# Graph attention and gated expert FFN on one core: how the attention stage broadcasts its scores and sums its rows

## The chip, the cores and the metric

The kernel runs on one core of one Trainium2 chip. The metric is the device time of one execution in microseconds (us). Three executions of the kernel before took 2421.63, 2421.95 and 2422.08 us; their median is 2421.95 us.

## The reference

There are 128 graphs of 128 nodes with 256 features each (`x`), and for every graph a 128x128 matrix of edge weights (`adj`). All of it is float32. What matters here is the attention layer:

```python
xn = layernorm(x)
Wh = xn @ W                              # 256 x 256
s1, s2 = Wh @ a[:256], Wh @ a[256:]
e = s1[:, :, None] + s2[:, None, :]      # a score for every pair of nodes
e = where(e > 0, e, 0.2 * e) + log(adj + 1e-6)
x = x + softmax(e, axis=-1) @ Wh
```

After it comes a feed-forward layer of 8 experts on the layer-normed result: three products with batch norm and relu for each expert, the experts' outputs weighted by a gate that is computed from the mean over the graphs. Its code is not touched.

## The kernel before

**Two stages.** The program has an attention stage, which goes over 32 groups of four graphs, and after a barrier the feed-forward stage over 32 tiles of 8 experts each. Everything that is changed lies in the attention stage, which takes about the first 285 us of 2419.

**What the attention stage computes for a group.** The weight of an edge is written without the logarithm: p = (adj + 1e-6) * exp(leaky(s1 + s2) - max), and the softmax's denominator is the sum of p over a row.
TensorE transposes x (L703, eight 128x128 blocks into PSUM), ScalarE copies that out as `xnT` (L561), and TensorE projects it (L734, into `ps_wide`); columns 256 and 257 of the projection are s1 and s2. ScalarE evicts the projection into `wh` (L548), scaled by the layer norm's factor.
s1 is a number per partition, so ScalarE can add it as a bias. s2 has to lie along the free dimension, the same on every partition. TensorE does that at L778: it takes a graph's s2 column, read as a 128x128 block in which the column is repeated, as the stationary operand, and the identity as the moving one. The result in `ps_s[i, j]` is s2[j] for every i. ScalarE adds s1 as it evicts it (L508, `s_sb`).
VectorE then forms the leaky relu (L636, `l_sb`), the negated row maximum (L645, `neg_m`), ScalarE the exponential (L528, `e_sb`, one instruction for each graph), VectorE the product with the adjacency (L674, `p_sb`, one instruction over all four graphs), and later the row sums (L686, `rowsum`, one reduction over all four graphs). TensorE transposes p (L771), ScalarE copies it out (L568, `pT`), and TensorE multiplies it with `wh` (L750, `ps_h`). VectorE takes the reciprocal of `rowsum` (L640, `rinv`), scales and adds the residual (L664, `x1`), and takes the statistics for the second layer norm (L588, L594).

**What sets the order.** Each engine has one in-order program, written by hand as `step(g, layer)`. In step g the engines work on several groups at once: a = g-1, b = g-2, t = g-3, h = g-4, and the next group, g+1. Semaphores tie the engines together. The first seven steps and the last four are written out, and the 24 between them are two hardware loops, the first of which also prepares weights of the feed-forward stage. TensorE's order in a step is: L750 for b, L734 for g, L703 for g+1, L771 for a, L778 for g. ScalarE's is: L508 for a, the scaling for the accumulation L516, L528 for a, L548 for g, L561 for g+1, L568 for a. VectorE's is: the accumulation L621 for h, L636 for a, L640 for b, L594 for t, L645 for a, L664 for b, L674 for a, L580 (statistics of x) for g+1, L588 for b (one graph), L686 for a, and L588 (the other three).

**The names that the change touches.** `p_done` counts finished products p: TensorE's L771 waits for it, and so do ScalarE's L528 and the load of `adj_sb` on the sync queue, both for older groups. `rowsum_done` counts finished row sums, and only VectorE waits for it, ahead of the reciprocal in the next step. `rinv_done` counts reciprocals; a row sum may be written over only when the reciprocal of the group before is taken.

Of the kernel before, what the change touches and what calls it, by code (L numbers as in the profile page):

```python
# [20 lines left out]
ALU = mybir.AluOpType  # L21
ACT = mybir.ActivationFunctionType
AX_X = mybir.AxisListType.X

P = 128
LN_EPS = 1e-5
ADJ_EPS = 1e-6
# [4 lines left out]
def wait(eng, sem, value):  # L32

    if isinstance(value, int) and value <= 0:
        return
    eng.wait_ge(sem, value)


def adj_ffn(nc, x, adj, gnn_w, gnn_a, wr, br, w1, b1, g1, be1, m1, v1, w2, b2, g2, be2, m2, v2, wo, bo, out):
    B, N, D = x.shape  # L40
    E = wr.shape[1]
    C = D // P
    GB = 4
# [13 lines left out]
    with ExitStack() as ctx:  # L57
# [3 lines left out]
        def sem(name, stack=ctx):  # L61
            return stack.enter_context(nc.semaphore(name))


        ident = sb("ident", [P, P])
# [119 lines left out]
        with ExitStack() as sa:  # L185
# [15 lines left out]
            adj_sb = [sba(f"adj_sb{i}", [P, GB, N]) for i in range(2)]  # L201
# [9 lines left out]
            wh = [sba(f"wh{i}", [P, GB, D + 2]) for i in range(2)]  # L211
# [3 lines left out]
            e_sb = sba("e_sb", [P, GB, N])  # L215
            p_sb = sba("p_sb", [P, GB, N])
            pT = sba("pT", [P, GB, N])
            rowsum = sba("rowsum", [P, GB])
# [10 lines left out]
            ps_s = ps("ps_s", [P, GB, N])  # L229
# [38 lines left out]
            p_done = sem("p_done", sa)  # L268
# [1 line left out]
            pT_copied = sem("pT_copied", sa)  # L270
            h_low_ready = sem("h_low_ready", sa)
            h_ready = sem("h_ready", sa)
            rowsum_done = sem("rowsum_done", sa)
            rinv_done = sem("rinv_done", sa)
            x1_low_done = sem("x1_low_done", sa)
            x1_done = sem("x1_done", sa)
# [12 lines left out]
            def num(g):  # L289
                return 2 * g[0] + g[1]  # L290
# [6 lines left out]
            def exists(g):  # L297
                return not isinstance(g[0], int) or 0 <= num(g) < G
# [276 lines left out]
            def _(dve):  # L575
# [16 lines left out]
                def aggregate_2(g):  # L592
                    for b4 in range(GB):
# [5 lines left out]
                                               in1=ps_wide[:, 0:1, 0:D].to_broadcast([P, C, D]), op0=ALU.mult,  # L599
                                               op1=ALU.subtract).then_inc(gw_centred, 1)  # L600

                def step(g, layer):
                    a = ago(g, 1)
                    b = ago(g, 2)
# [22 lines left out]
                    add_part(0)  # L627
                    add_part(1)
                    if exists(b):
                        dve.wait_ge(rowsum_done, num(b) + 1)  # L630
                    if exists(t):
                        dve.wait_ge(bnst2, num(t) + 1)
                    if exists(a):
# [36 lines left out]
                    if exists(a):  # L670
                        dve.wait_ge(e_done, num(a) + 1)
                        dve.wait_ge(adj_loaded[r], 16 * (a[0] + 1))
                        wait(dve, pT_ready, num(a))
                        nc.vector.scalar_tensor_tensor(out=p_sb[:, :, :], in0=adj_sb[r][:, :, :], scalar=ADJ_EPS,  # L674
                                                       in1=e_sb[:, :, :], op0=ALU.add,
                                                       op1=ALU.mult).then_inc(p_done, 1)
                    if exists(nxt):
                        wait(dve, rstd1_done, num(nxt) - 1)
                        for b4 in range(GB):
                            stats_1(nxt, b4)  # L680
                    if with_stats:
                        stats_2(b, 0)
                    if exists(a):
                        dve.wait_ge(p_done, num(a) + 1)
                        wait(dve, rinv_done, num(a))
                        nc.vector.tensor_reduce(rowsum[:, :], p_sb[:, :, :], AX_X, ALU.add).then_inc(rowsum_done, 1)  # L686
                    if with_stats:
                        for b4 in range(1, GB):
                            stats_2(b, b4)
# [6 lines left out]
            @block.tensor  # L696
            def _(pe):
                def next_rows(g):
                    pe.wait_ge(x_loaded[g[1]], 16 * (g[0] + 1))
                    for c in range(C):  # L700
                        wait(pe, (x1_low_done, x1_done)[c], num(ago(g, 3)) + 1)
                        for b4 in range(GB):
                            last = nc.tensor.transpose(ps_xT[:, c, b4 * N:(b4 + 1) * N],  # L703
                                                       x_sb[g[1]][:, b4, c * P:(c + 1) * P], ident[:, :])
                    last.then_inc(xnT_ready, 1)

                pe.wait_ge(setup_done, 1)
                next_rows((0, 0))
                pe.wait_ge(mean_w_set, 1)
                pe.wait_ge(proj_loaded, 2 * 16)  # L710
                for c in range(C):
                    last = nc.tensor.matmul(ps_wide[:, 0, 0:D], mean_w[:, :], gw[:, c, 0:D], start=(c == 0),
                                            stop=(c == C - 1))
                last.then_inc(col_mean_ready, 1)
                pe.wait_ge(gw_centred, 1)

                for m in range(C):
                    for c in range(C):
                        nc.tensor.transpose(ps_wide[:, 1 + m, c * P:(c + 1) * P], gw[:, c, m * P:(m + 1) * P], ident[:, :])
                nc.tensor.transpose(ps_s[:, 0, 0:2 * C], a_rows[:, :], ident[0:2 * C, 0:2 * C]).then_inc(proj_T, 1)  # L720
                pe.wait_ge(proj_T_copied, 1)

                a_pair = a_cols[:, :].rearrange("p (k m) -> p m k", k=2)
                for c in range(C):
                    for m in range(C):
                        last = nc.tensor.matmul(ps_s[:, 1, 2 * c:2 * c + 2], gwT[:, m, c * P:(c + 1) * P],
                                                a_pair[:, m, :], start=(m == 0), stop=(m == C - 1))
                last.then_inc(va_ready, 1)

                def project(g, graphs):  # L730

                    for b4 in graphs:
                        for c in range(C):
                            mm = nc.tensor.matmul(ps_wide[:, b4, 0:D + 2], xnT[:, c, b4 * N:(b4 + 1) * N],  # L734
                                                  gw[:, c, :], start=(c == 0), stop=(c == C - 1))
                    return mm

                def step(g, layer):
                    a = ago(g, 1)
                    b = ago(g, 2)  # L740
                    nxt = ago(g, -1)
                    if exists(b):

                        pe.wait_ge(pT_copied, num(b) + 1)
                        wait(pe, x1_done, num(b))
                        pe.wait_ge(xnT_copied, min(num(g) + 1, G) if isinstance(g[0], int) else num(g) + 1)
                        if is_step(g, G):
                            pe.wait_ge(xs_copied, 1)
                        for b4 in range(GB):
                            last = nc.tensor.matmul(ps_h[:, b4, :], pT[:, b4, :], wh[b[1]][:, b4, 0:D], start=True,  # L750
                                                    stop=True)
                            if b4 == HB - 1:
                                last.then_inc(h_low_ready, 1)
                        last.then_inc(h_ready, 1)
                    if is_step(g, 0):
                        pe.wait_ge(va_copied, 1)
                    if exists(g):
                        pe.wait_ge(xnT_copied, num(g) + 1)
                        wait(pe, wh_copied, num(g))
                        project(g, range(HB)).then_inc(wh_ready, 1)  # L760
                        project(g, range(HB, GB)).then_inc(wh_ready, 1)
                    if is_step(g, G - 1):
                        pe.wait_ge(x1_done, num(b) + 1)
                        tile_transpose(pe, 0, ps_x0)
                    if exists(nxt) and not is_step(nxt, 0):
                        next_rows(nxt)
                    if exists(a):
                        pe.wait_ge(p_done, num(a) + 1)
                        wait(pe, pT_copied, num(a))
                        for b4 in range(GB):  # L770
                            last = nc.tensor.transpose(ps_pT[:, b4, :], p_sb[:, b4, :], ident[:, :])  # L771
                        last.then_inc(pT_ready, 1)
                    if exists(g):

                        pe.wait_ge(wh_copied, num(g) + 1)
                        wait(pe, s_done, num(g))
                        for b4 in range(GB):
                            last = nc.tensor.matmul(ps_s[:, b4, :], wh[g[1]][:, b4, D + 1:D + 2].to_broadcast([P, P]),  # L778
                                                    ident[:, :], start=True, stop=True)
                        last.then_inc(s2b_ready, 1)  # L780
                    if is_step(g, BN_STEP - 1):
                        pe.wait_ge(small_loaded, 16 * N_SMALL)
                        for r in range(10):
                            last = nc.tensor.transpose(ps_bn[:, r, :], bn_rows[:, r // 5, r % 5, :],
                                                       ident[0:EC, 0:EC])
                        last.then_inc(bn_T, 1)

                over_groups(pe, step)


# [490 lines left out]
```

## Time and profile before

| | |
|---|---|
| median of three runs | 2421.95 us |
| the profiled execution's own time | 2421.09 us |
| its span in the profile | 2419.3 us |
| TensorE busy | 2382.8 us (98%), 16292 instructions |
| VectorE busy | 1691.5 us (70%) |
| ScalarE busy | 1618.1 us (67%) |
| GpSimd busy | 417.0 us (17%) |

The span runs from the first to the last instruction of one execution, and the execution's own time is 1.8 us more. The busy shares are means over two stages that differ: the feed-forward stage is about seven eighths of the time, and TensorE is all but always busy there. So the page's totals say little about the attention stage, and its rows were asked for by stretches of time. Instructions of one engine overlap by their fill and drain: the step from one start to the next is shorter than the duration.

### The profile page before, as it was taken

Reading aid. Unit: us, or ns where it says so; the run is one execution under the profiler, and the core shown is the slowest. Engines: PE = TensorE matmul, PEld = TensorE weight load, DVE = VectorE, ACT = ScalarE, POOL = GpSimd, SP = SyncE. Lnnn points to the kernel's source line nnn. Section 1 sums busy time; section 2 is a strip of 40 time slices with the busy share of each in tenths; the row PEclk is TensorE's granted clock in tenths of the full one; section 3 lists DMA queues with packets and bytes.
Section 4 is the critical chain, followed back from the end, with each engine's and each line's share of the span. In section 5 each row is a group of like instructions: output and inputs, shape, how many; then the busy total and the mean of one; then the engine's idle time right before and its main releaser. Section 6 shows DMA issues by size and latency. Waiting matters only on the chain.

```text
span 2419.3 us, 45995 instructions
## 1 busy us (share of the span) xinstructions
PE 2382.8 (98%) x16292; PEld 2206.4 (91%) x16292; DVE 1691.5 (70%) x2509; ACT 1618.1 (67%) x2524; POOL 417.0 (17%) x553
## 2 busy tenths in 40 slices
PE   8999899999999999999999999999999999999999
PEld 7888689999999999999999999999999999999998
DVE  5999866666666666666666666666666666666666
ACT  5888676666666666666666666666666666666665
POOL 4777521111101011111111101011111111001010
PEclk9999899999999999999999999999999999999999
DMA  5777410000000000000000000000000000000000
GB/s 184 245 239 260 156 36 27 26 26 26 26 26 24 20 9 26 26 26 26 26 26 26 26 26 17 20 14 26 26 26 26 26 26 26 26 26 17 17 10 27
DMA packets 91178, 116.16 MB, mean 48 GB/s; under 512 B 4700, under 2 KB 78856, under 8 KB 91144
## 3 DMA queue, kind: packets, MB, share of 16 engines
q1 hardware_dynamic: 91144, 115.73, 14.4%
q8 instruction: 19, 0.31, 0.1%
q14 instruction: 15, 0.12, 0.0%
HBM read 82.16 MB, written 33.55 MB: 48 GB/s over the span
## 4 chain that ended last, share of the span: by engine, by line
PE 88%; DVE 0%; ACT 0%; issue 0%
PE ps_y L1189 30%; PE ps_wide L171 30%; PE ps_wide L1170 27%; PE ps_t L132 1%; DVE h_lo L1074 0%; DVE z L1067 0%; ACT h_hi L969 0%; ACT v L974 0%; DVE resb L1097 0%; DVE h_lo L1080 0%; DVE z L1057 0%; PE ps_t L1234 0%; PE ps_t L1216 0%; PE ps_t L1221 0%; ACT featT L1000 0%
## 5 line engine op out<-in xcount | busy, mean ns | idle before, releaser
L974 ACT ACTIVATE v<-ps_wide,bn_cols 128x256 f32<-128x256 f32 x768 | 433.9, 565 | 394.9 <-PE ps_wide L1170 258.7
L982 ACT ACTIVATE h<-ps_wide,bn_cols 128x512 f32<-128x512 f32 x512 | 399.0, 779 | 325.4 <-PE ps_wide L171 323.2
L1189 PE MATMUL ps_y<-wo_lo,h_hi 128*128 128x256 f32 x2048 | 578.8, 283 | 0.0
L1189 PE MATMUL ps_y<-wo_hi,h_lo 128*128 128x256 f32 x2048 | 578.3, 282 | 0.0
L1189 PE MATMUL ps_y<-wo_hi,h_hi 128*128 128x256 f32 x2048 | 577.2, 282 | 0.5 <-DVE h_lo L1080 0.5
L1074 DVE SCALAR_TENSOR_TENSOR h_lo<-z,h_hi 128x1024 fp32r<-128x1024 f32 x256 | 313.7, 1225 | 341.7 <-ACT h_hi L969 341.7
L1170 PE MATMUL ps_wide<-xq_hi,wq_hi 128*128 128x256 f32 x1792 | 506.0, 282 | 7.6 <-PEq L185 3.3
L1170 PE MATMUL ps_wide<-xq_lo,wq_hi 128*128 128x256 f32 x1792 | 509.5, 284 | 0.0
L1170 PE MATMUL ps_wide<-xq_hi,wq_lo 128*128 128x256 f32 x1792 | 506.8, 283 | 0.0
L171 PE MATMUL ps_wide<-h_lo,w_hi 128*128 128x512 f32 x1024 | 405.6, 396 | 0.0
L171 PE MATMUL ps_wide<-h_hi,w_lo 128*128 128x512 f32 x1024 | 405.4, 396 | 0.0
L171 PE MATMUL ps_wide<-h_hi,w_hi 128*128 128x512 f32 x1024 | 404.1, 395 | 0.5 <-DVE h_lo L1074 0.5
L1189 PEld LDWEIGHTS ps_y<-wo_hi,h_hi 128*128 128x128 f32 x2048 | 386.5, 189 | 1.1 <-DVE h_lo L1080 0.7
L1189 PEld LDWEIGHTS ps_y<-wo_hi,h_lo 128*128 128x128 f32 x2048 | 387.4, 189 | 0.0
L1189 PEld LDWEIGHTS ps_y<-wo_lo,h_hi 128*128 128x128 f32 x2048 | 386.5, 189 | 0.0
L1080 DVE TENSOR_TENSOR h_lo<-h,h_hi 128x1024 fp32r<-128x1024 f32 x256 | 313.4, 1224 | 95.5 <-ACT h_hi L988 95.5
L1170 PEld LDWEIGHTS ps_wide<-xq_hi,wq_hi 128*128 128x128 f32 x1792 | 340.9, 190 | 20.1 <-issue 4.0
L953 POOL TENSOR_TENSOR resb<-resb,w_bc 128x512 f32<-128x512 f32 x64 | 86.8, 1357 | 1570.5 <-DMA resb<-x_scratch 1563.5
L1170 PEld LDWEIGHTS ps_wide<-xq_hi,wq_lo 128*128 128x128 f32 x1792 | 338.2, 189 | 10.0
L1170 PEld LDWEIGHTS ps_wide<-xq_lo,wq_hi 128*128 128x128 f32 x1792 | 339.8, 190 | 0.0
L1097 DVE SCALAR_TENSOR_TENSOR resb<-ps_y,w_node,resb 128x512 f32<-128x512 f32 x448 | 333.1, 743 | 3.9 <-PE ps_y L1189 3.9
L1067 DVE SCALAR_TENSOR_TENSOR z<-ps_wide,bn_cols,v 128x512 f32<-128x512 f32 x256 | 191.9, 750 | 178.2 <-PE ps_wide L1170 178.2
(132 smaller groups left out, 3002.4 us busy)
## 6 DMA issues: line engine op xcount, KB each, us to landing
x_sb<-in_x SPq DMA_DIRECT2D x32, 512.0 KB, 4.0
res<-in_x SPq DMA_DIRECT2D x32, 512.0 KB, 5.8
x1t<-x_scratch SPq DMA_DIRECT2D x32, 512.0 KB, 3.2
resb<-x_scratch SPq DMA_DIRECT2D x32, 512.0 KB, 3.3
out<-resb SPq DMA_DIRECT2D x32, 512.0 KB, 3.0
adj_sb<-in_adj SPq DMA_DIRECT2D x32, 256.0 KB, 6.1
x_scratch<-h SPq DMA_DIRECT2D x16, 512.0 KB, 4.8
x_scratch<-w_bc SPq DMA_DIRECT2D x16, 512.0 KB, 4.6
```

Of the source, the lines that this page charges most:

```text
L132: last = nc.tensor.transpose(ps_x[:, c, b4 * N:(b4 + 1) * N], x1t[:, b4, c * P:(c + 1) * P], ident[:, :])
L171: mm = nc.tensor.matmul(acc_ps, w[:, i, c, cols], s[:, c, :], start=start and n == 0, stop=stop and n == len(terms) - 1)
L953: nc.gpsimd.tensor_tensor(resb[:, g, :], resb[:, g, :], ysum[:, g, :], ALU.add).then_inc(resb_done, 1)
L974: nc.scalar.activation(v[:, slot, :], ps_l1[:, 0, 0:H], ACT.Identity, bias=bn_cols[:, 1, cols], scale=bn_cols[:, 0, cols]).then_inc(done, 1)
L982: nc.scalar.activation(h2[:, m, :], ps_l2[:, m, :], ACT.Relu, bias=bn_cols[:, 3, cols], scale=bn_cols[:, 2, cols]).then_inc(r2_done, 1)
L1067: nc.vector.scalar_tensor_tensor(out=z[:, 0, :], in0=ps_l1[:, 1, :], scalar=bn_cols[:, 0, C * e:C * e + 1], in1=v[:, 0:2, :].rearrange("p ...
L1074: nc.vector.scalar_tensor_tensor(out=h1_lo[:, :, :], in0=z[:, :, :], scalar=0.0, in1=h1_hi[:, :, :].bitcast(F32), op0=ALU.max, op1=ALU.sub ...
L1080: nc.vector.tensor_tensor(h2_lo[u[1] % 2][:, :, :], h2[:, :, :], h2_hi[u[1] % 2][:, :, :].bitcast(F32), ALU.subtract).then_inc(lo2_done, 1)
L1097: nc.vector.scalar_tensor_tensor(out=dst[:, g, :], in0=ps_y[:, g, :], scalar=w_node[:, e:e + 1], in1=old, op0=ALU.mult, op1=ALU.add).then_ ...
L1170: mm = nc.tensor.matmul(out_ps, w[:, e, q, :], x[:, q, :], start=start and n == 0, stop=stop and n == len(terms) - 1, skip_group_check=True)
L1189: mm = nc.tensor.matmul(ps_y[:, b4, :], h[:, c, cols], w[:, e, c, :], start=(k == 0 and b4 % per_bank == 0), stop=(k == len(terms) - 1 and ...
```

## The change

TensorE's four matmuls with the identity become four transposes of the same repeated column, which give the same block. The reduction of p is taken out: the product p is done as four instructions of one graph each, and each gives its row sums from the instruction's accumulator output. With that, `rowsum_done` goes, the reciprocal waits for `p_done` in its place, and the wait for the reciprocal of the group before moves from the reduction to the product. Where each remaining instruction stands in its engine's order is as before.

```diff
@@ VectorE, ahead of L636
                     if exists(b):
-                        dve.wait_ge(rowsum_done, num(b) + 1)
+                        dve.wait_ge(p_done, num(b) + 1)
@@ VectorE, L674
-                        nc.vector.scalar_tensor_tensor(out=p_sb[:, :, :], in0=adj_sb[r][:, :, :], scalar=ADJ_EPS,
-                                                       in1=e_sb[:, :, :], op0=ALU.add,
-                                                       op1=ALU.mult).then_inc(p_done, 1)
+                        wait(dve, rinv_done, num(a))
+                        for b4 in range(GB):
+                            last = nc.vector.scalar_tensor_tensor(out=p_sb[:, b4, :], in0=adj_sb[r][:, b4, :],
+                                                                  scalar=ADJ_EPS, in1=e_sb[:, b4, :], op0=ALU.add,
+                                                                  op1=ALU.mult, accum_out=rowsum[:, b4:b4 + 1])
+                        last.then_inc(p_done, 1)
@@ VectorE, L686
-                    if exists(a):
-                        dve.wait_ge(p_done, num(a) + 1)
-                        wait(dve, rinv_done, num(a))
-                        nc.vector.tensor_reduce(rowsum[:, :], p_sb[:, :, :], AX_X, ALU.add).then_inc(rowsum_done, 1)
@@ TensorE, L778
-                            last = nc.tensor.matmul(ps_s[:, b4, :], wh[g[1]][:, b4, D + 1:D + 2].to_broadcast([P, P]),
-                                                    ident[:, :], start=True, stop=True)
+                            last = nc.tensor.transpose(ps_s[:, b4, :],
+                                                       wh[g[1]][:, b4, D + 1:D + 2].to_broadcast([P, P]), ident[:, :])
```

## Rows read from the trace of the kernel before

**Rows 1.** Steady stretch: us; busy PE, PEld, DVE, ACT, POOL; granted clock; DMA share, GB/s.

```profile
60.00:240.00 180.00, 170.17 (x977) 149.93 (x977) 172.93 (x512) 150.05 (x393) 137.89 (x248) 1.00 0.76 247
```

**Rows 2.** Timeline of one step, TensorE and ScalarE; start, duration, instruction, [idle before].

```profile
127.83 3.65 PE L734 MATMUL ps_wide<-gw,xnT 128*128 128x258 f32 x16
...
131.52 0.84 ACT L548 ACTIVATE wh<-ps_wide,rstd 128x258 f32<-128x258 f32 x2 [0.75 <-PE ps_wide L734]
...
132.19 0.60 PE L771 MATMUL ps_pT<-ident,p_sb 128*128 128x128 f32 x4
...
132.47 1.02 ACT L561 ACTIVATE xnT<-ps_th 128x1024 f32<-128x1024 f32 x1
...
132.63 1.06 PE L778 MATMUL ps_s<-ident,wh 128*128 128x128 f32 x8
...
133.39 0.59 ACT L568 ACTIVATE pT<-ps_pT 128x512 f32<-128x512 f32 x1
...
133.87 1.15 ACT L508 ACTIVATE s_sb<-ps_s,wh 128x128 f32<-128x128 f32 x4
...
134.12 1.99 PE L750 MATMUL ps_th<-wh,pT 128*128 128x256 f32 x8 [0.43 <-ACT pT L568]
...
135.94 3.65 PE L734 MATMUL ps_wide<-gw,xnT 128*128 128x258 f32 x16
```

**Rows 3.** Timeline of VectorE in the step that follows.

```profile
135.05 0.69 DVE L636 SCALAR_TENSOR_TENSOR l_sb<-s_sb 128x512 f32<-128x512 f32 x1 [0.33 <-ACT s_sb L508]
...
135.75 0.35 DVE L594 BATCH_NORM_AGGREGATE mv<-st 128x2 f32<-128x6 f32 x4
...
136.01 0.65 DVE L645 TENSOR_REDUCE neg_m<-l_sb 128x4 f32<-128x512 f32 x1
136.58 1.65 DVE L664 SCALAR_TENSOR_TENSOR w_bc<-ps_th,rinv,res 128x256 f32<-128x256 f32 x4
...
138.15 0.68 DVE L674 SCALAR_TENSOR_TENSOR p_sb<-adj_sb,e_sb 128x512 f32<-128x512 f32 x1
...
138.75 1.39 DVE L580 BATCH_NORM_STATS2 st<-x_sb 128x6 f32<-128x256 f32 x4
...
140.06 0.41 DVE L588 BATCH_NORM_STATS2 st<-w_bc 128x6 f32<-128x256 f32 x1
...
140.39 0.67 DVE L686 TENSOR_REDUCE rowsum<-p_sb 128x4 f32<-128x512 f32 x1
...
140.97 1.07 DVE L588 BATCH_NORM_STATS2 st<-w_bc 128x6 f32<-128x256 f32 x3
```

**Rows 4.** Waits from 60 to 240 us: who waited for whom, total, times, longest.

```profile
PE ps_th L750 <- ACT pT L568: 9.8, 23, 0.4
```

**Rows 5.** The same view from 10 to 290 us.

```profile
DVE l_sb L636 <- ACT s_sb L508: 21.0, 29, 10.8
```

**Rows 6.** Groups by line, 60 to 240 us; busy us, mean ns of one.

```profile
L778 PE MATMUL ps_s<-ident,wh 128*128 128x128 f32 x183 | 24.2, 275 | 0.0
...
L771 PE MATMUL ps_pT<-ident,p_sb 128*128 128x128 f32 x88 | 13.2, 273 | 0.0
```

**Rows 7.** Timeline of the end of the attention stage.

```profile
276.49 0.75 DVE L674 SCALAR_TENSOR_TENSOR p_sb<-adj_sb,e_sb 128x512 f32<-128x512 f32 x1
...
278.63 3.78 PE L750 MATMUL ps_th<-wh,pT 128*128 128x256 f32 x8 [0.69 <-ACT pT L568]
...
283.28 1.62 DVE L664 SCALAR_TENSOR_TENSOR w_bc<-ps_th,rinv,res 128x256 f32<-128x256 f32 x4
```

**Rows 8.** Timeline of TensorE's first work.

```profile
4.46 1.94 PE L703 MATMUL ps_th<-ident,x_sb 128*128 128x128 f32 x8 [4.46 <-DMA x_sb<-in_x]
...
6.20 1.91 PE L712 MATMUL ps_wide<-gw,mean_w 128*128 128x256 f32 x4
...
8.89 0.66 PE L719 MATMUL ps_wide<-ident,gw 128*128 128x128 f32 x4 [0.78 <-DVE gw L598]
```

**Rows 9.** TensorE by stretch: us, PE busy (x), granted clock, DMA share, GB/s.

```profile
285.70:301.60 15.90, 12.90 (x46) 0.50 0.40 133
```

More of the change, by code:

```diff
@@ L272, in adj_ffn @@
             h_ready = sem("h_ready", sa)
-            rowsum_done = sem("rowsum_done", sa)
             rinv_done = sem("rinv_done", sa)
```

## The prediction

> **What bounds the kernel now.** I first read the busy times by stretch, because both edits lie in the first 285 us and the page's totals are mostly of the other stage. In the steady part TensorE is busy for 170.17 of 180 us and VectorE for 172.93 [rows 1]. The reader is to see that two engines are near full at once, so that busy time alone can't say which one sets the end. A faster TensorE or a faster VectorE would be worth something only if it stood in the loop that closes last.
>
> So I took the timeline of one step and followed it round. The projection L734 starts at 127.83 and again at 135.94: a step is 8.11 us. In it TensorE finishes L734 at 131.48; ScalarE evicts its second half at 131.52 (0.84 us), having been idle 0.75 us for it; ScalarE then copies xnT from 132.47 (1.02 us) and pT from 133.39 to 133.98; TensorE starts L750 at 134.12, having been idle 0.43 us for it, and gets to L734 again 1.82 us later [rows 2]. That ring is 3.65 + 0.04 + 0.95 + 0.92 + 0.73 + 1.82 = 8.11 us, the whole step. Every wait in it is real. The view of waits says the same for the stretch: L750 waited 23 times for pT, 9.8 us or 0.43 us each [rows 4].
>
> L778, the first thing to be changed, is not in the ring. TensorE runs it from 132.63 to 133.69, in the time in which ScalarE makes xnT and pT, and is idle afterwards [rows 2]. Nor is its result: ScalarE's eviction of it, L508, starts at 133.87, right behind pT, and not when L778 is done.
>
> VectorE, where the second edit lies, has one gap in a step: 0.33 us before L636, in which it waits for the last of L508 (133.87 + 1.15 = 135.02, and L636 starts at 135.05) [rows 2, 3]. From 10 to 290 us it made that wait 29 times out of 32 groups [rows 5]. So VectorE follows ScalarE with 0.33 us to spare, and its own work is 8.11 - 0.33 = 7.78 us a step.
>
> **The scores by transpose.** A float32 matmul shows as two records here and a transpose as one: L778 has 183 records in a stretch in which L771, which is also four blocks a group, has 88. 183 records are busy for 24.2 us, 0.132 us each; L771's 88 for 13.2 us, 0.150 us each [rows 6]. By the timeline, L778 takes 1.06 us a step and L771 0.60 us [rows 2]. The edit takes four records of eight away, 1.06 - 0.60 = 0.46 us of TensorE a step, or 14.7 us over 32 groups. Its worth is the part that reaches the ring, and that is nothing: TensorE would stop at 133.23 in place of 133.69, and L750 still starts 0.14 us behind pT at 133.98. The idle time before L750 grows from 0.43 to 0.89 us. Nothing waits for the earlier score. I take 0; the least is also 0, unless the whole 14.7 us came through (a rival below), and the most is what a lower clock would cost (another).
>
> **The product in four parts.** VectorE's work is priced by the step from one start to the next. Now: L674 to L580 is 138.75 - 138.15 = 0.60 us, and the reduction L686 to the next statistics 140.97 - 140.39 = 0.58 us, together 1.18 us [rows 3]. Later: four instructions of 128 elements with an accumulator output, 4X. The trace has none of them. A 256-element statistic steps by (140.06 - 138.75)/4 = 0.33 us, and a 6-element aggregate by (136.01 - 135.75)/4 = 0.065 us; the line through both gives 0.065 + 122 x 0.00106 = 0.19 us for 128 elements, which I round to 0.20 for the product alone. If the accumulator costs nothing, X = 0.20. If it costs as much as another tiny instruction, X = 0.20 + 0.07 = 0.27. If the read-out has to wait until its product is through, X is the product's full duration plus a small one's: 0.20 + 0.08 (the duration of L674, 0.68, less its step of 0.60) + 0.16 (a lone small instruction: L594's four take 0.35, less three steps of 0.065) = 0.44. The far end is the step of a 256-element instruction with two more operands, L664's (138.15 - 136.58)/4 = 0.39, plus the same 0.16: X = 0.55. I take 0.27, which is nearest to the small instructions of the rows; the range keeps 0.20 to 0.55.
>
> The Trainium skill (VectorE: DVE Perf Modes, section "Two Vector instructions with no wait between them") says that an op that also writes its accumulator out is two instructions, the main one and a read of the accumulator. No row of before shows one. By that rule the 0.20 end is out, and 0.27 or more stands; the sum below does not change.
>
> With X = 0.27 the change on VectorE is 4 x 0.27 - 1.18 = -0.10 us a step. In a step with a gap that only widens the gap, to 0.43 us. The gap is used up at 4X = 1.18 + 0.33, X = 0.38.
>
> **What moves with it.** p is complete, and `p_done` is raised, at 138.15 + 4 x 0.27 + 0.08 = 139.31 in place of 138.83. TensorE comes to L771 at 132.19 + 8.11 = 140.30 [rows 2, 3], so the later product is hidden with 1.0 us to spare; even X = 0.55 makes it 140.43, 0.1 us late. What stands behind L771 on TensorE is L778 and L750, and pT on ScalarE. ScalarE's exponential and the load of the adjacency wait for the product of an older group, a step ago. The wait for `rinv_done` that is now ahead of the product was met in the same step: the reciprocal comes before L645, over 2 us earlier. The reciprocal's new wait, for `p_done`, is for a product of a step ago. Everything between the product and the old place of the reduction (five statistics) starts 4 x 0.27 - 0.60 = 0.48 us later and gets it back, and 0.10 more, where the reduction was; GpSimd's work on x's statistics has its own slack. No DMA is moved.
>
> **The end of the stage.** In the last steps VectorE has no gap: three of 32 groups show no such wait for scores [rows 5], two of them at the end. I count two places at which VectorE's own sum is the end, of -0.10 us each. In the last one TensorE waits for the product itself; there the change delays L771, pT and L750 by 0.4 us. L750 would end at 278.63 + 3.78 + 0.4 = 282.8, and VectorE needs its second half only at the third instruction of L664, 283.28 + 0.8 = 284.1 [rows 7]. It is covered by 1.3 us.
>
> **Sum.** 30 steps at 0, two at -0.10: -0.2 us. The profiled execution took 2421.09 us, so 2420.9; it lay 0.9 us under the median of 2421.95, so the median should be 2421.8 us. The feed-forward stage starts with a clock of 0.50 for 15.9 us [rows 9], and where in that stretch the clock comes back may shift by more than 0.2 us makes one think; I allow 3 us on either side for it. The likeliest case's own range is 2418.5 to 2425.
>
> **Rival 1, slower: the accumulator's read makes VectorE the bound.** If X is over 0.38, VectorE's work exceeds the 8.11 us ring, and each step grows by 4X - 1.51. The 24 steps in the hardware loops are the ones I count, and two at the end that pay all of 4X - 1.18. At X = 0.44: 24 x 0.25 + 2 x 0.58 = 7.2 us, 2429 us. At X = 0.55: 24 x 0.69 + 2 x 1.02 = 18.6 us, 2441 us. For it: VectorE is at 96% already, and four instructions have four fills and drains. Against it: the read has to cost more than twice what the smallest instructions of the rows cost. Chance 0.16.
>
> **Rival 2, slower: the clock.** TensorE loses 0.46 us of work a step, and four real matmuls become transposes. From the end of L734 at 131.48 to L750 at 134.12 it would then do transposes and nothing else, 2.64 us of each 8.11. If transposes did not keep the clock up, it would fall from time to time to 1.2 GHz. L750 takes 3.78 us there in place of 1.99 [rows 2, 7], 1.8 us more in each step that meets it; in half of the steps, 16 x 1.8 = 29 us, 2451 us. Against it stands the start: TensorE did eight transposes in 1.94 us and four matmuls in 1.91, 0.24 us a transpose, and then four transposes in 0.66 us, which is the full clock's speed (L771: 0.60) [rows 2, 8]. After the barrier it was busy with matmuls alone for 12.90 of 15.9 us and stayed at 0.50 [rows 9]. A stretch that was half transposes raised the clock where 81% of matmuls did not. Chance 0.06.
>
> The Trainium skill (TensorE: Matmul & The Clock Gate, section "Part 4: PE-mode transpose") speaks for this rival: a transpose does not count as TensorE being busy in the way a matmul does, so the full clock doesn't engage for it. The start of this trace speaks against that, in the numbers just given.
>
> **Rival 3, faster: TensorE's saving comes through.** If L778 did hold up L750, for instance through the order in which TensorE takes up queued work, up to 14.7 us would come back: 2407 us. Against it: in 23 of 23 steps L750's wait ended with pT. Chance 0.04.
>
> **Numbers.** The forecast has 0.74, and all of its time lies within 0.2% (4.8 us, about what a measurement of this kernel can tell from no change). Rivals 1 and 2 have 0.22 and rival 3 0.04. Of rival 1, a third lies between X = 0.38 and 0.41, under 4.8 us and so within 0.2%. That makes 0.04 faster, 0.79 within, 0.17 slower. The range is 2418 to 2431 us: the forecast, and rival 1 up to X = 0.46.
>
> **What would show it.** Right: L778 with half its records and about 0.6 us a step, the wait of L750 for pT grown to about 0.9 us, L734 to L734 still 8.11 us, and VectorE's gap before L636 near 0.4 us. Wrong on VectorE: no gap before L636, ScalarE waiting longer for L645, and steps of more than 8.11 us. Wrong on the clock: a granted clock under 1.00 between 30 and 250 us. Wrong on the ring: L734 to L734 under 8.1 us.

## The result, and the profile after

The changed kernel takes 2427.90 us (median of 19 executions, 2424.85 to 2430.33); the kernel before 2421.95 us (19 executions, 2420.57 to 2423.28). The ratio is 1.0022, with a 95% interval of 1.0016 to 1.0029: 6 us slower, where 2421.8 us and no measurable change was forecast. The time lies in the range of 2418 to 2431 us, but the likeliest case was the wrong one.

The steady stretch after, in the columns of [rows 1]:

```profile
60.00:240.00 180.00, 157.69 (x856) 133.32 (x855) 176.47 (x617) 144.72 (x379) 136.61 (x240) 1.00 0.74 239
```

TensorE is busy for 12.5 us less in the same 180 us and VectorE for 3.5 us more, at a clock of 1.00. Fewer instructions went through on ScalarE (379 for 393), so the stretch holds less work: the steps are longer. The waits of the same stretch answer to [rows 4]:

```profile
PE ps_th L748 <- ACT pT L567: 12.8, 22, 0.9
PE ps_pT L769 <- DVE p_sb L675: 8.9, 8, 1.2
...
DVE l_sb L635 <- ACT s_sb L507: 3.5, 6, 0.7
```

The middle row is new. Eight times in 180 us TensorE waited up to 1.2 us for the product p, which the prediction had ready 1.0 us ahead of TensorE. VectorE's wait for the scores is left in 6 steps. The groups of lines, as in [rows 6], show what became longer:

```profile
L675 DVE SCALAR_TENSOR_TENSOR p_sb<-adj_sb,e_sb 128x128 f32<-128x128 f32 x84 | 38.1, 506 | 0.0
...
L776 PE MATMUL ps_s<-ident,wh 128*128 128x128 f32 x88 | 13.3, 273 | 0.1
...
L675 DVE DVE_READ_ACCUMULATOR p_sb<-adj_sb,e_sb 128x1 f32 x84 | 6.6, 78 | 0.0
```

L776 has lost half its records, as forecast. The accumulator's read is an instruction of 78 ns. But a part of the product takes 506 ns in the mean, and that mean hides two kinds. One step of the timeline shows them, as [rows 3] did:

```profile
142.19 0.28 DVE L675 SCALAR_TENSOR_TENSOR p_sb<-adj_sb,e_sb 128x128 f32<-128x128 f32 x1
142.40 0.08 DVE L675 DVE_READ_ACCUMULATOR p_sb<-adj_sb,e_sb 128x1 f32 x1
142.40 0.28 DVE L675 SCALAR_TENSOR_TENSOR p_sb<-adj_sb,e_sb 128x128 f32<-128x128 f32 x1
142.48 2.15 POOL L470 TENSOR_TENSOR wq_lo<-w_stage,wq_hi 128x896 f32 x1 [0.20 <-POOL rstd_all L451]
...
142.61 2.16 DVE L675 SCALAR_TENSOR_TENSOR p_sb<-adj_sb,e_sb 128x128 f32<-128x128 f32 x1
...
144.70 0.28 DVE L675 SCALAR_TENSOR_TENSOR p_sb<-adj_sb,e_sb 128x128 f32<-128x128 f32 x1
...
145.05 0.66 PE L769 MATMUL ps_pT<-ident,p_sb 128*128 128x128 f32 x4 [1.18 <-DVE p_sb L675]
```

A part takes 0.28 us and steps by 0.21 us, until GpSimd starts its `wq_lo` at 142.48. The third part, issued at 142.61, ends at 144.77, 0.14 us after GpSimd's instruction (144.63). It was held for 1.88 us (2.16 less 0.28), and TensorE was idle for 1.18 us ahead of L769. In the other step of each pair, GpSimd's four sums of about 0.5 us hold two parts to 0.53 and 0.54 us.

TensorE's projection, to set beside the 8.11 us of [rows 2]:

```profile
131.23 3.65 PE L732 MATMUL ps_wide<-gw,xnT 128*128 128x258 f32 x16
...
139.34 3.65 PE L732 MATMUL ps_wide<-gw,xnT 128*128 128x258 f32 x16
...
148.29 3.65 PE L732 MATMUL ps_wide<-gw,xnT 128*128 128x258 f32 x16
```

That is 8.11 and 8.95 us, 17.06 us for a pair of steps in place of 16.22. In this stretch VectorE is the bound (busy for 144.21 of the 145 us from 60 to 205): two steps of its own work and the holds, 1.88 + 0.26 + 0.25, make up the pair. Where no part is held and VectorE sets the pace, near the end, the product starts at 268.44 and 275.78, so its own work is 7.34 us a step; 2 x 7.34 + 2.39 = 17.07 us. From the sixth product to the 24th, 18 steps, it takes 152.38 us after and 145.98 before: 6.4 us, which covers the 6 us of the medians. In the steps in which GpSimd has only `w_lo` to do, no part is held and the step is 8.11 us again (the first of them, 7.45 us, makes up for some of the last hold).

### The profile page after: what moved, and what is told of

The parts are those of the page before. It is cut to its first block, busy times and chain, and to the rows that moved or that the text cites. A ratio compares the mean times of both kernels' runs of the same rounds, so it can differ in the third digit from the quotient of the medians.

```text
span 2428.6 us, 45931 instructions
## 1 busy us (share of the span) xinstructions
PE 2374.4 (98%) x16164; PEld 2192.3 (90%) x16164; DVE 1698.7 (70%) x2701; ACT 1618.4 (67%) x2524; POOL 420.5 (17%) x553
## 4 chain that ended last, share of the span: by engine, by line
PE 87%; DVE 1%; ACT 0%; issue 0%; DVEq 0%; ACTq 0%
PE ps_y L1187 30%; PE ps_wide L171 29%; PE ps_wide L1168 26%; PE ps_t L132 1%; DVE z L1065 0%; DVE x1t L124 0%; ACT h_hi L967 0%; DVE feat_sum L1105 0%; DVE resb L179 0%; DVE z L1055 0%; DVE resb L1095 0%; DVE h_lo L1072 0%; ACT v L972 0%; DVE h_lo L1078 0%; PE ps_t L1227 0%
```

## The experiments

Each ratio is against the kernel before, timed beside the variant at medians of 2422.2 to 2422.3 us.

**E1, the transposes alone.**

```diff
-last = nc.tensor.matmul(ps_s[:, b4, :], wh[g[1]][:, b4, D + 1:D + 2].to_broadcast([P, P]), ident[:, :], ...)
+last = nc.tensor.transpose(ps_s[:, b4, :], wh[g[1]][:, b4, D + 1:D + 2].to_broadcast([P, P]), ident[:, :])
```

> The scores by transposes, VectorE's edit left out. Both theories put the whole loss on VectorE and expect no change against before, 2422 us within 2 us, with TensorE's wait for pT grown from 0.43 to about 0.9 us a step and the clock at 1.00. If transposes cost clock or start-up time, some of the 6 us shows here.

Measured: 2421.67 us, ratio 0.9995 (0.9986 to 1.0004). The wait row of its steady stretch:

```profile
PE ps_th L750 <- ACT pT L568: 19.4, 22, 0.9
```

19.4 us for 22 waits is 0.88 us, where 0.89 was forecast. What TensorE saves, it waits. The clock was 1.00 there, so the transposes cost nothing by that way either.

**E2, the accumulator alone**: the changed kernel with `matmul` back in its place at L776.

> The product in four parts with accumulator outputs, the scores still by matmuls. Both theories expect all of the loss, 5 to 7 us over before (2427 to 2429 us). If the transposes had a hand in it, it is less than that.

Measured: 2427.88 us, 1.0025 (1.0015 to 1.0036). The whole loss is VectorE's edit.

**E3, the split alone.**

```diff
-nc.vector.scalar_tensor_tensor(out=p_sb[:, :, :], in0=adj_sb[r][:, :, :], ...).then_inc(p_done, 1)
+for b4 in range(GB):
+    last = nc.vector.scalar_tensor_tensor(out=p_sb[:, b4, :], in0=adj_sb[r][:, b4, :], ...)
+last.then_inc(p_done, 1)
```

> The product in four parts without accumulator outputs, the reduction kept, the scores by matmuls. Theory 1 (a part of the product that starts while GpSimd is in a long instruction waits until that one is through, as the third part did behind wq_lo, 2.16 us): the same parts are held, and VectorE has 0.33 us a step more to do than in the changed kernel, so at least 6 us over before, more likely 8 to 14. Theory 2 (the accumulator output and its read cause the stall): no long part, VectorE has 4 x 0.21 + 0.58 = 1.42 us in place of 1.18, inside its gap of 0.33 us, so 2422 us within 2 us.

Measured: 2423.48 us, 1.0006 (0.9997 to 1.0015). Theory 1 as I had put it failed: four parts alone lose nothing that can be measured. The trace shows the meeting with GpSimd all the same, and who loses it (four parts merged in one row):

```profile
138.03 0.89 DVE L675 SCALAR_TENSOR_TENSOR p_sb<-adj_sb,e_sb 128x128 f32<-128x128 f32 x4
138.60 2.27 POOL L471 TENSOR_TENSOR wq_lo<-w_stage,wq_hi 128x896 f32 x1 [0.20 <-POOL rstd_all L452]
```

GpSimd starts inside the product again, but its instruction is the one that is longer, 2.27 us for 2.10, and no part is held. That includes the fourth part, which starts at 138.03 + 3 x 0.20 = 138.63, just behind GpSimd's start. So parts that follow each other without a break keep GpSimd out. The accumulator's read would be the break.

**E4, GpSimd behind the product.** In the changed kernel, three waits in GpSimd's program:

```diff
 pool.wait_ge(w_loaded, 32 * (e + 1))
+pool.wait_ge(p_done, num(ago(g, 1)) + 1)
...
 pool.wait_ge(wq_hi_done, e + 1)
+pool.wait_ge(p_done, num(ago(g, 1)) + 1)
...
 pool.wait_ge(w_hi_done, i + 1)
+pool.wait_ge(p_done, num(ago(g, 1)) + 1)
```

> The changed kernel, with GpSimd's work on the feed-forward weights (the four sums, wq_lo and w_lo) made to wait until the product is done. Theory 1: no part of the product is held, all take 0.28 us, steps are 8.11 us again, and the time is that of before, 2421 to 2423 us. Theory 2 (accumulator) and a third (four instructions are simply more than one): no change against the changed kernel, 2427 to 2429 us.

Measured: 2420.66 us, 0.9996 (0.9987 to 1.0005). The accumulator reads are all there, all parts take 0.28 or 0.29 us, and every step of the loops is 8.10 to 8.12 us. The loss is gone with the meeting alone. VectorE's wait for L508 shows what the change saves where nothing is held:

```profile
DVE l_sb L638 <- ACT s_sb L510: 15.3, 23, 0.7
```

That is 0.67 us a step, where the kernel before had 0.33.

**E5, something small between the parts.** E3, with

```diff
 for b4 in range(GB):
+    if b4:
+        nc.vector.tensor_reduce(between[:, b4:b4 + 1], e_sb[:, b4, 0:4], AX_X, ALU.add)
     last = nc.vector.scalar_tensor_tensor(...)
```

> The product in four parts without accumulator outputs, the reduction kept, and between each two parts a small reduction of 4 elements whose result nobody reads. The split alone cost 1.2 us and held no part: GpSimd's wq_lo, started at 0.57 us after the first part, was held instead (2.26 us for 2.10). Theory 1a (anything that stands between two parts lets a waiting GpSimd instruction in, and the next part is held for its whole length): parts of 2.1 us as in the changed kernel, steps over 8.11 us, 6 to 15 us over before. Theory 1b (only the accumulator's read does): no part over 0.3 us; VectorE has about 1.6 us in place of 1.18, 0.1 us a step beyond its gap, so 1 to 4 us over before.

Measured: 2450.02 us, 1.0117 (1.0102 to 1.0132), more than either theory gave. The timeline decides between them:

```profile
147.84 0.27 DVE L678 SCALAR_TENSOR_TENSOR p_sb<-adj_sb,e_sb 128x128 f32<-128x128 f32 x1
147.85 2.20 POOL L472 TENSOR_TENSOR wq_lo<-w_stage,wq_hi 128x896 f32 x1 [0.20 <-POOL rstd_all L453]
148.04 0.14 DVE L677 TENSOR_REDUCE between<-e_sb 128x1 f32<-128x4 f32 x1
148.10 2.09 DVE L678 SCALAR_TENSOR_TENSOR p_sb<-adj_sb,e_sb 128x128 f32<-128x128 f32 x1
```

Theory 1a: a small instruction that is no accumulator read lets GpSimd in just as well. The size was off since the fourth part now starts late enough to meet `w_lo` too:

```profile
222.24 1.30 POOL L477 TENSOR_TENSOR w_lo<-w_stage,w_hi 128x512 f32 x1 [0.55 <-ACT w_hi L540]
...
222.40 1.29 DVE L678 SCALAR_TENSOR_TENSOR p_sb<-adj_sb,e_sb 128x128 f32<-128x128 f32 x1
```

These steps are 9.09 us and the pairs with `wq_lo` 18.4 us. In the changed kernel `w_lo` starts at 0.63 to 0.66 us after the first part, and the last part at 0.63: it gets by.

**E6, one input out of SBUF.** The changed kernel with the exponential written over the scores in PSUM:

```diff
-            e_sb = sba("e_sb", [P, GB, N])
...
             ps_s = ps("ps_s", [P, GB, N])
+            e_sb = ps_s
```

> The changed kernel with the exponential written to PSUM, over the scores that are no longer needed, so that a part of the product has one input in SBUF in place of two. GpSimd's work stands where it was. If a part is held because both its inputs are in SBUF while GpSimd reads there, no part is held now, steps are 8.11 us and the time is 2420 to 2423 us. If any VectorE instruction that meets GpSimd's is held, the long parts stay: 2427 to 2429 us.

Measured: 2421.47 us, 0.9999 (0.9990 to 1.0008). GpSimd starts in the middle of the product as before, and nobody is held:

```profile
137.84 0.28 DVE L675 SCALAR_TENSOR_TENSOR p_sb<-adj_sb,ps_s 128x128 f32<-128x128 f32 x1
138.00 2.09 POOL L470 TENSOR_TENSOR wq_lo<-w_stage,wq_hi 128x896 f32 x1 [0.20 <-POOL rstd_all L451]
138.05 0.08 DVE L675 DVE_READ_ACCUMULATOR p_sb<-adj_sb,ps_s 128x1 f32 x1
138.05 0.28 DVE L675 SCALAR_TENSOR_TENSOR p_sb<-adj_sb,ps_s 128x128 f32<-128x128 f32 x1
```

So it takes both: two inputs in SBUF, and an instruction of GpSimd under way when the part starts.

**E9, only the longest one behind the product.** E4 with the wait at `wq_lo` alone.

> The changed kernel with only GpSimd's longest instruction, wq_lo (2.1 us, 8 times), made to wait for the product. The four sums may still hold two parts by 0.26 us each, which VectorE's gap of about 0.66 us takes up. If a hold costs only what it has beyond the gap, all of the loss is wq_lo's: steps of 8.11 us, 2420 to 2423 us. If every hold costs, a quarter of the loss or more stays: 2424 us or over.

Measured: 2420.49 us, 0.9995 (0.9986 to 1.0004). The sums still hold one part in each second step:

```profile
144.85 0.29 DVE L676 SCALAR_TENSOR_TENSOR p_sb<-adj_sb,e_sb 128x128 f32<-128x128 f32 x1
144.96 0.49 POOL L458 TENSOR_TENSOR w_stage<-w_stage 128x128 f32<-128x128 f32 x1 [0.16 <-POOL rstd_all L451]
145.06 0.08 DVE L676 DVE_READ_ACCUMULATOR p_sb<-adj_sb,e_sb 128x1 f32 x1
145.06 0.54 DVE L676 SCALAR_TENSOR_TENSOR p_sb<-adj_sb,e_sb 128x128 f32<-128x128 f32 x1
```

0.25 us fits into VectorE's gap and costs nothing; the steps are 8.11 us. The whole loss hangs on eight instructions of GpSimd.

**E7, E8 and E10, the ring.** If the ring of the prediction sets the step, shortening it must show. ScalarE's copy `xnT` is cut in two, the second half behind pT; L750's first half waits for pT and the first half, its second for the rest (E7 on E4, E8 on the kernel before, E10 on E6):

```diff
-nc.scalar.activation(xnT[:, :, :], ps_xT, ACT.Copy).then_inc(xnT_copied, 1)
+nc.scalar.activation(xnT[:, 0, :], ps_xT[:, 0, :], ACT.Copy).then_inc(xnT_low, 1)
...
 nc.scalar.activation(pT[:, :, :], ps_pT[:, :, :], ACT.Copy).then_inc(pT_copied, 1)
+nc.scalar.activation(xnT[:, 1, :], ps_xT[:, 1, :], ACT.Copy).then_inc(xnT_copied, 1)
```

> The changed kernel with GpSimd behind the product, and ScalarE's copy xnT in two halves: the first before pT, the second behind it, so that the first half of L750 starts 0.4 us earlier. If the ring of L734, the second half of wh, xnT, pT and L750 sets the step, as the prediction said, it falls from 8.11 to about 7.7 us, and 28 steps give 11 us: 2408 to 2413 us. If something else does, no change against 2421 us.

> The kernel before, with the copy xnT in two halves in the same way. The ring would allow 7.7 us, but VectorE has 7.78 us of work a step: 7.8 us, 9 us under before, 2411 to 2415 us, and 1 to 3 us over the changed kernel with the same edit.

> The changed kernel with the exponential in PSUM (no part can be held) and the copy xnT in two halves, GpSimd's work where it was. With GpSimd behind the product, 14 steps stayed at 7.96 us because GpSimd ran late into the next product. Here it does not: all steps 7.69 us, 14 x 0.27 = 4 us under that kernel, 2406 to 2409 us. If VectorE's own work is the next bound, above 7.69 us, it stays at 2411 us.

Measured: E7 2411.31 us, 0.9959 (0.9945 to 0.9973); E8 2412.70 us, 0.9961 (0.9948 to 0.9975); E10 2409.10 us, 0.9945 (0.9932 to 0.9959). In the loops E8's steps are 7.68 us throughout, not 7.8, and E10's 7.68 to 7.69. E7 begins so, but from its tenth product on the first part is held in 14 products, and 12 steps take 7.94 to 7.98 us:

```profile
140.90 1.27 POOL L441 TENSOR_TENSOR resb<-resb,x1s_high 128x512 f32<-128x512 f32 x1
141.56 0.76 DVE L682 SCALAR_TENSOR_TENSOR p_sb<-adj_sb,e_sb 128x128 f32<-128x128 f32 x1
```

GpSimd, put off by its wait, ran late and came into the next product with another instruction; this time the first part was held. E10 has no such meeting, since its product reads one input from PSUM. It is 13 us faster than the kernel before, the best version here, though the 2.2 us that it gains over E7 are fewer than the 4 expected (E7's longer steps cost 3.3 us in all, not 14 x 0.27 = 4). Its waits say what sets the step:

```profile
PE ps_th L755 <- ACT pT L569: 11.0, 24, 0.5
DVE l_sb L639 <- ACT s_sb L509: 6.2, 23, 0.3
```

TensorE still waits 0.46 us a step and VectorE 0.27, so neither is full, and the ring sets the 7.68 us. E8 gains 9.5 of these 13 us on the kernel before, so most of the credit is the ring's. But in E8 TensorE is busy for 179.68 us of 180 and VectorE for 180.00: there the shorter ring has used up what both had to spare, and by these figures a still shorter one would be worth nothing without the two savings of the change. The change's own part, E10 against E8, is a few us, which these runs don't separate well.

## Why the prediction was wrong

**The ring** was right. E1, E4, E6 and E9 all keep 8.11 us whatever TensorE or VectorE saves. E8 and E10 take it to 7.68 or 7.69, as forecast for the shorter ring, and E7 does where no part is held.

**The scores by transpose** at 0 was right, with its growth of the wait from 0.43 to 0.88 us (E1). Rival 3, that the saving comes through, and rival 2, the clock, both fell with that run: 0.9995 at a clock of 1.00. The Trainium skill's rule on transposes that the prediction cites for rival 2 is not borne out here. E1 is also better evidence on the clock than the start of the trace, which the prediction read from durations: the granted clock stands at 1.00 there (4.4 to 8.2 us), so its rows show no rise.

**The product in four parts.** X is 0.21 us, under the 0.27 taken and at the floor of the range. By its own work VectorE gained 1.18 - 4 x 0.21 = 0.34 us a step, not 0.10, and has 7.34 us of it. The 7.78 us given for before was 0.1 us too much: E8 runs at 7.68 with VectorE never idle. The gap of 0.33 us is counted from the end of the instruction ahead, while back to back the next one starts about 0.08 us before that end (L674's 0.68 less 0.60). The Trainium skill's rule that an op with an accumulator output is two instructions (VectorE: DVE Perf Modes, "Two Vector instructions with no wait between them") holds: the read has its own rows, of 0.08 us. What the prediction drew from it, that X would be 0.27 or more, does not: the read starts together with the next part, and the step grows by 0.01 us.

**Rival 1** had the sign and, by chance, the size (2429 us at X = 0.44), but not the mechanism. It wanted a costly read in every step; the read is nearly free, and the steps with `w_lo` did not grow. The signs that the prediction gave for it came all the same: VectorE's gap gone but in 6 steps, ScalarE's wait for L645 grown from 12.5 to 23.5 us in the steady stretch, steps over 8.11 us. They tell that VectorE is the bound, not why.

**What moves with it** is the step that failed: "GpSimd's work on x's statistics has its own slack", and "the later product is hidden with 1.0 us to spare". It priced a part of the product at X and put the meeting with GpSimd at nothing. The runs showed a hold of 1.88 us in each of eight steps and two of 0.25 us in the steps between, which made 17.06 us of a pair of steps that had taken 16.22. I asked what waits for the later product, and which semaphores it waits for, and not what else runs while it does. The trace of before had the answer in a row that I did not use:

```profile
138.72 2.10 POOL L471 TENSOR_TENSOR wq_lo<-w_stage,wq_hi 128x896 f32 x1 [0.20 <-POOL rstd_all L452]
```

It starts 0.57 us after the start of the product [rows 3]. Before, the product was one instruction that had started first and was all but through: `wq_lo` takes 2.10 us, and 2.09 in E6, where nobody is held. In four parts with a read after each, the fourth part starts at 0.63 us, behind GpSimd, and is held. After the first hold the two drift: in the next steps with `wq_lo` it starts 0.28 us after the first part, and the third part is held.

The end of the stage even had such a hold in it, which I did not see:

```profile
280.02 2.30 POOL L441 TENSOR_TENSOR resb<-resb,x1s_high 128x512 f32<-128x512 f32 x1 [1.64 <-issue]
281.13 1.88 DVE L621 SCALAR_TENSOR_TENSOR resb<-w_bc,rstd_all,resb 128x256 f32<-128x256 f32 x2
```

L621 takes 0.86 us elsewhere (two instructions), and it also has two inputs in SBUF.

The Trainium skill states this rule (SBUF — State Buffer, "SBUF: two separate sides"): VectorE and GpSimd share a port pair under an exclusive lock; a VectorE op with two SBUF inputs, against a GpSimd op that reads SBUF, blocks fully if the other started first. The traces agree where GpSimd is in first: the held part takes 2.16 us beside an instruction of 2.15, and with one input in PSUM there is no hold (E6). They differ from it in one thing: in E3 the fourth part starts behind `wq_lo` and it is still GpSimd that is held, so VectorE keeps its place over instructions that follow each other without a break. Read ahead of the prediction, with the row above, the rule would have given it a further rival: eight holds of up to 2 us, less VectorE's gaps.

**The end of the stage** gained more than the -0.1 us a step: 7.34 and 7.35 us between its last products, for 7.69 and 7.38 before. The profiled execution of the changed kernel is 2.4 us over its median, and its feed-forward stage 3 us longer than that of before. Most of this is the clock, for which 3 us had been allowed: in the 34 us behind the barrier it was 0.50 for 16 us and then 1.00 before, and 0.68 and then 0.72 after, 26.0 against 23.8 us at full clock. These are single executions.

## What to carry to other kernels

Splitting an instruction can cost more than its extra fills: each seam with something else in it, if only an accumulator's read, is a place where another engine can take what the whole instruction held. Before cutting a VectorE operation with two SBUF inputs, look at which GpSimd instructions start within its time in the present trace, and price a hold of their full length for each. If the cut is wanted, move one input to PSUM, or let GpSimd wait, and in that case check where its work runs into next. And when two engines look full, walk the ring first: 0.42 us a step taken out of it gave 9.5 us (E8), where 0.46 us of TensorE and 0.34 us of VectorE off it gave nothing that could be measured (E1, E6).

## What the runs showed of the hardware

- Four VectorE instructions with two SBUF inputs, back to back at steps of 0.20 us, keep GpSimd out until the last of them, even one that starts 0.03 us behind GpSimd (E3: `wq_lo` 2.27 us for 2.10). One small instruction in between, of 0.08 or 0.14 us, lets it in, and the next part is then held behind `wq_lo` for 1.8 us or more (the changed kernel, E5). One whole product does the same as four in a row: where `wq_lo` starts 0.29 us into it (E8), it takes 2.35 us.
- An accumulator output costs almost nothing by itself: parts with it step by 0.21 us, and E3's four without it take 0.80 us from first start to the next instruction.
- With L778 as transposes too, TensorE does nothing but transposes between L734 and L750, 16 records a step, and then idles for 0.88 us. The granted clock was still 1.00 from 60 to 240 us (E1).
